# The last cross attention of a decoder: where the causal mask is added to the scores

## The reference

```
q = (queries @ Wq + bq).reshape(B, L, H, dk)      # queries: layernorm(x), 16 x 112 x 256; H = 16, dk = 16
k = (keys @ Wk + bk).reshape(B, S, H, dk)         # keys, values: the context
v = (values @ Wv + bv).reshape(B, S, H, dk)
scores = jnp.einsum('blhd,bshd->bhls', q, k)
causal = jnp.triu(jnp.ones((L, S), dtype=bool), k=1)
scores = jnp.where(causal[None, None], -jnp.inf, scores)
attn = jax.nn.softmax(scores / sqrt(dk), axis=-1)
out = jnp.einsum('bhls,bshd->blhd', attn, v).reshape(B, L, H * dk) @ Wo + bo
```

## Time and profile before

| | us |
|---|---|
| median of three runs | 1831.58 |
| profiled execution | 1840.86 |
| its span | 1839.1 |
| TensorE busy in the span | 1663.2 (90%) |
| VectorE busy | 925.9 (50%) |
| ScalarE busy | 870.3 (47%) |
| GpSimd busy | 336.3 (18%) |

### The profile page before, as it was taken

The page is one execution under the profiler, slowest core; times in us unless marked ns, Lnnn a source line. Parts: engine busy times, 40 slices in busy tenths (PEclk is TensorE's granted clock), DMA queues, the critical chain, the costliest instruction groups (busy, mean ns, idle before and its releaser), DMA issues. The chain is left out here.

```text
span 1839.1 us, 32803 instructions
## 1 busy us (share of the span) xinstructions
PE 1663.2 (90%) x12682; PEld 1091.1 (59%) x12682; DVE 925.9 (50%) x1898; ACT 870.3 (47%) x1780; POOL 336.3 (18%) x304
## 2 busy tenths in 40 slices
PE   7999999799889999989899999999797988699965
PEld 3455555555456656656565899998354666466632
DVE  5566666321656665656433211211464766377747
ACT  5243434333555565665431122222265878256655
POOL 0012112121100000000008400001702544101112
PEclk9999999899999999999979999999897999799978
DMA  7000000100200000000025599996378331000001
GB/s 246 1 1 1 1 1 1 48 5 1 80 18 18 10 18 18 10 18 2 2 65 203 181 330 328 323 330 206 113 181 203 89 83 42 21 12 12 2 1 41
DMA packets 147914, 150.03 MB, mean 82 GB/s; under 512 B 69760, under 2 KB 134976, under 8 KB 147760
## 3 DMA queue, kind: packets, MB, share of 16 engines
q1 hardware_dynamic: 144688, 140.59, 25.0%
q0 software_dynamic: 3072, 7.34, 1.3%
HBM read 120.39 MB, written 27.53 MB: 80 GB/s over the span
## 5 line engine op out<-in xcount | busy, mean ns | idle before, releaser
L906 DVE CUSTOM_DVE_ANT_0 x_probs<-psum,masked 112x439 f32<-112x439 f32 x256 | 142.1, 612 | 71.5 <-PE psum L748 70.7
L759 PE MATMUL psum<-ident,x_probs 112*125 112x112 f32 (+1 forms) x1024 | 142.6, 278 | 28.4 <-DVE x_turned L913 24.6
L759 PEld LDWEIGHTS psum<-ident,x_probs 112*125 112x125 f32 (+1 forms) x1024 | 117.2, 169 | 85.7 <-issue 40.2
L846 ACT ACTIVATE x_probs<-x_probs,x_negmax 112x439 f32<-112x439 f32 x256 | 155.1, 658 | 8.2 <-DVE x_negmax L906 8.2
L2302 DVE TENSOR_TENSOR masked<-masked 128x512 f32<-128x512 f32 x70 | 49.9, 712 | 200.9 <-ACT masked L2204 200.9
L2145 PEld LDWEIGHTS psum<-mix_xb,mix_up 128*128 128x128 f32 x1120 | 130.6, 192 | 2.1 <-issue 0.4
L2145 PE MATMUL psum<-mix_xb,mix_up 128*128 128x128 f32 x1120 | 130.7, 275 | 0.0
L852 ACT COPY x_turned<-psum 125x448 f32<-125x448 f32 x128 | 67.8, 530 | 129.9 <-PE psum L759 128.9
L2155 PE MATMUL psum<-mix_down,masked 128*128 128x256 f32 x560 | 127.0, 380 | 0.1
L1389 PE MATMUL psum<-fold_full,hT 128*112 128x512 f32 x256 | 113.8, 597 | 1.3 <-DVE fold_part L1697 1.3
L2155 PEld LDWEIGHTS psum<-mix_down,masked 128*128 128x128 f32 x560 | 103.5, 190 | 13.4 <-DVE masked L2302 0.4
(11 more groups left out here) (320 smaller groups left out, 3278.7 us busy)
## 6 DMA issues: line engine op xcount, KB each, us to landing
mix_up<-in_moe_up SPq DMA_DIRECT2D x35, 1024.0 KB
mix_down<-in_moe_down SPq DMA_DIRECT2D x35, 1024.0 KB
offset_rows<-join_rows SPq DMA_DIRECT2D x16, 784.0 KB, 5.9
hrow<-offset_rows SPq DMA_DIRECT2D x16, 784.0 KB, 5.3
x_ctx<-in_ctxT SPq DMA_DIRECT2D x16, 375.0 KB, 3.1
slots_x<-masked SPq DMA_DIRECT2D x1, 4480.0 KB, 21.4
mix_rows<-slots_x SPq DMA_DIRECT2D x35, 128.0 KB, 3.0
slots_y<-mix_result SPq DMA_DIRECT2D x35, 128.0 KB, 3.3
```

The lines of the kernel that those rows point to most:

```text
L759: mm = nc.tensor.transpose(psum[0:CHUNK_ROWS[c], 4 + i % 2, k * T:(k + 1) * T], probs[:, n % 2, slot_of_head(HG * g + k), c * CHUNK:c * CH ...
L846: nc.scalar.activation(probs[:, n % 2, slot], probs[:, n % 2, slot], ACT.Exp, bias=negmax[:, n % 2, slot:slot + 1], scale=-1.0).then_inc(e ...
L906: nc.vector.tensor_tensor_reduce(probs[:, n % 2, slot], psum[0:T, slot % 4, 0:KEYS], masked[0:T, n * KEYS:(n + 1) * KEYS], -1.0, -3.0 * NE ...
```

## The change

VectorE now adds the mask, and TensorE no longer does in this stage. In each block of four heads, VectorE runs one `tensor_tensor_reduce` per head in the place of the one maximum per block. It reads the 112 columns of the head's scores from PSUM, adds the mask, multiplies by -1 and writes the result, the negated masked score, to `probs` in SBUF; with the same instruction it finds the minimum over the columns, which is the negated maximum, and a second small instruction writes it to `rowmax`. (With the factor -1 and the starting value 3e30 for the minimum this is the form that the memory attention has already, in `mask_and_largest`, L902, with 439 columns.) `shift` then takes the negated scores from SBUF instead of the scores from PSUM, and ScalarE's exponent has a scale of -1.

On TensorE the mask products are gone from this stage; the first attention keeps them. The score products are the first into their banks (start=True). Since VectorE's first instruction has the scores out of PSUM, the banks are free after `maxed` instead of `shifted`. The new instruction writes `probs`, so it waits for the turns of batch n-2, as `shift` does.

```diff
-        banks_free = factored if offset else shifted
+        banks_free = factored if offset else maxed if causal else shifted
...
-                    if not offset:
+                    if future:
                         nc.tensor.matmul(psum[0:T, r, 0:G], identb[0:T, 0:T], maskb[:], start=True, stop=False, skip_group_check=True)
...
-                        mm = nc.tensor.matmul(psum[0:T, r, k * T:(k + 1) * T], q, kT[rows, g % 2, m, t:t + T], start=offset, stop=True, skip_group_check=not offset)
+                        mm = nc.tensor.matmul(psum[0:T, r, k * T:(k + 1) * T], q, kT[rows, g % 2, m, t:t + T], start=not future, stop=True, skip_group_check=future)
...
-                nc.scalar.activation(x, x, ACT.Exp).then_inc(exped.sem, 1)
+                nc.scalar.activation(x, x, ACT.Exp, scale=-1.0 if causal else 1.0).then_inc(exped.sem, 1)
...
+                elif causal:
+                    dve.wait_ge(*scored.after(At(n), r))
+                    dve.wait_ge(*tile_turned.after(At(n - 2), NG - 1))
+                    for k in range(HG):
+                        found = nc.vector.tensor_tensor_reduce(x[:, k], src[:, k], maskb[:, 0:T], -1.0, -3.0 * NEG, ALU.add, ALU.min, mx[:, k:k + 1])
+                    found.then_inc(maxed.sem, 1)
                 else:
                     dve.wait_ge(*scored.after(At(n), r))
                     nc.vector.tensor_reduce(mx, src, X, ALU.max).then_inc(maxed.sem, 1)
...
-                nc.vector.tensor_tensor(x, src, mx.unsqueeze(2).broadcast_to([T, NG, T]), ALU.subtract).then_inc(shifted.sem, 1)
+                nc.vector.tensor_tensor(x, x if causal else src, mx.unsqueeze(2).broadcast_to([T, NG, T]), ALU.subtract).then_inc(shifted.sem, 1)
```

## The result

The kernel before took 1834.51 us (median of 20 runs), the changed one 1841.7 (20 runs): ratio 1.0042 [1.0027, 1.0056], about 7.7 us slower. That is inside the 0.5% that I called no change, but the interval excludes both no change at all and the small gain that I forecast (1829.5). The time lies in the range of 1822 to 1842, but by luck: the upper end was set for a case, 263 ns per small instruction, that isn't what happened.

The account below looks back on a forecast made before the run. TensorE was taken to set the stage's pace, with VectorE close behind; mask products saved, less VectorE's longer chain (+1.0 us per batch), summed over the batches to -2.2 us, from 1831.6 to 1829.4 (predicted 1829.5), range 1822 to 1842.

Parts of the forecast that it names:

- a case, 263 ns per small instruction: VectorE's small instructions with one fixed part each for instruction and read: +9 us, 1840.7; under a rival of chance 0.18.
- The rival I gave most weight: VectorE's accumulator reads at 112 columns are not hidden: 263 ns gives +9 us, 354 gives +24; chance 0.18.
- the step between the small instructions: VectorE's 112-column mask-and-maximum instructions, with their reads, come 0.197 us apart.
- the chain: VectorE's work per batch, first maximum to next work: four blocks and the shuffle, 6.31 us instead of 5.31.
- The mask's time: TensorE gets back 0.85 us per batch from the removed mask products, at most 13.6 us over 16 batches.
- The walk's three hand-overs: Logarithm, third copy and third mix wait for VectorE's shuffle; output for centring (batches 7, 11, 15); next scores for last block.
- the walk: Batch-by-batch reckoning of the stage: TensorE's mask saving against VectorE's delays, summing to -2.2 us.
- The centring's wait ahead of the output: In batches 7, 11 and 15 TensorE's output waits for VectorE's centring: +0.1 us each, +1.0 in 15.
- new waits for the last maximum: TensorE's next scores wait for VectorE's last maximum, starting 6.88 us after the last ones at the earliest.
- it stays at 0.54: VectorE's subtraction, now reading SBUF instead of PSUM, was taken to keep its 0.54 us.
- One or two of these, +3 to +7: TensorE's clock drops to 1.2 GHz around batches 7, 11, 12, 14: +3 to +7 us; part of the within-0.5% chance, 0.76.
- a step of 0.247: VectorE's small instructions 0.247 us apart instead of 0.197: the walk comes out at +5.5 us.

Follow-up runs that it names:

- e4: Changed kernel with the 64 mask products kept on TensorE beside VectorE's mask; 1.0079 against the kernel before, stage 176.19 us.
- h2: Changed kernel with GpSimd's multiplication cut to 8 columns and useless TensorE products in batches 1 and 2; 1.0009 against the kernel before, stage 160.86 us.
- e2: Changed kernel with GpSimd's multiplication by the inverse denominators cut from 448 columns to 8; 1.0018 against the kernel before, stage 163.45 us.
- e1: Changed kernel with the masked scores written back to PSUM and subtracted from there; 1.006 against the kernel before, stage 168.48 us.
- g1: Changed kernel with only the row maxima put in spare PSUM columns, masked scores in SBUF; 1.0055 against the kernel before, stage 168.27 us.
- g3: Changed kernel with useless TensorE products in pauses at batches 1, 2 and 9; 1.0018 against the kernel before, stage 165.74 us.
- e3: Kernel before without the 64 mask products and without any mask; 0.9972 against the kernel before, stage 155.64 us.
- g2: Changed kernel with row maxima in PSUM and the denominators' shuffle ahead of block 0; 1.0024 against the kernel before, stage 166.17 us.
- h1: Changed kernel with shuffle first, last two subtractions after their maxima, GpSimd's multiplication held back in some batches, useless products before batch 1; 0.9961 against before, stage 154.22 us.
- g4: Changed kernel with row maxima in PSUM, shuffle ahead of block 0, and eight useless products ahead of batch 1's scores; 1.002 against before, stage 165.35 us.
- e6: Kernel before with the shuffle of the denominators moved ahead of block 0 on VectorE; 0.9967 against the kernel before, stage 154.89 us.
- f1: Changed kernel with the shuffle of the denominators moved ahead of block 0 on VectorE; 1.0003 against the kernel before, stage 165.42 us.

## Why the prediction was wrong

**Right.** The rival I gave most weight, that the second instruction of each head counts in full, is false: the step between the small instructions is 0.195 (forecast 0.197), the block 1.43 (1.44), the chain 6.40 (6.31) with one subtraction of 0.73 in it. The mask's time was right (0.85 forecast; 0.7 to 0.8 in e4, 0.87 ahead of batch 0). The walk's three hand-overs hold: where the two causes below are away (h2), the batches without a meeting are within 0.2 us of the walk except 13, which is 0.5 shorter because its output no longer waits for the multiplication that the edit cuts. The centring's wait ahead of the output, new waits for the last maximum, and VectorE's higher busy time are there.

**The step that failed:** "The subtraction now reads SBUF instead of PSUM; with two inputs it has no row at another rate here, so it stays at 0.54." Rate was the wrong question. At 0.54 alone, it takes 1.34 when it comes while GpSimd works on SBUF, because both its operands are there now. It costs 4.3 us (e2, less what its edit brings by itself), and some 1.6 more where the partner is the sum of squares (batches 6, 10 and 14 over the walk in e2 and h2), through three of the walk's hand-overs: later banks (12 and 14: 7.74 for 6.88), later queries (5), and the third copy in 9. And the trace of before had rows that show it. By line, VectorE's normalisation step with two SBUF operands and GpSimd's addition of the bias:

```profile
L285 DVE TENSOR_TENSOR hT<-hT,sq x24: 1081/1092/1981, 222.2 to 1775.3; 128x896 f32<-128x896 f32 x24
```

```profile
L1849 POOL TENSOR_TENSOR second_result<-second_result,weights x32: 1127/1448/1472, 1406.1 to 1558.8; 112x448 f32<-112x448 f32 x32
```

VectorE's step reaches 1981 at a median of 1092, GpSimd's addition has 1127 at the least and 1448 at the median, and neither reads PSUM. Their places in the trace fit: the step of 1981 starts 0.10 us after a GpSimd multiplication of 1.14, and the 18 additions of 1445 ns or more all start 0.16 us after a VectorE addition with two SBUF operands, while none of the other 14 (at most 1147 ns) does. I read means and steps of VectorE, never the spread, and looked for no row of GpSimd at all. That 14 multiplications stood beside the chain before too and lengthened no subtraction is explained by its PSUM operand: the same is shown by e1 and g1.

The Trainium skill ("SBUF — State Buffer", "SBUF: two separate sides") has the rule: VectorE and GpSimd share a pair of ports that is "an exclusive lock, not a bandwidth split", and a VectorE instruction with two SBUF inputs and a GpSimd one that reads SBUF block each other for the whole instruction, whichever starts first. The trace agrees: GpSimd's instruction runs from 1677.63 to 1678.77, the subtraction is recorded from 1677.82, and the work behind it starts at 1679.17, within 0.15 us of 1678.77 + 0.54; and where GpSimd comes second it is the one that takes longer (its sum of squares in batches 6, 10 and 14 takes 1.51 instead of 1.14).

**The clock.** The second failed step: this was a rival ("One or two of these, +3 to +7") that I left out of the sum, and it came true: 3.4 us in batches 1 and 2 (g3), 1.5 at the end (an output of 4.76 for 3.29). I placed it at 7, 11, 12 and 14; it came in 1, 2, 9 and 15. The longest waits of TensorE there are 2.0 (ahead of batch 1's scores), 1.5, 1.8 and 3.3 us, where before they were 0.8, 0.6, 0.6 and 1.65. e3 shows that it needs nothing of VectorE's new work, nor a meeting. The length of one wait alone doesn't decide: the scores of batches 13 and 15 wait 1.7 and keep the clock, those of batch 15 in g2 wait 2.4 and keep it, and in e3 it falls behind a wait of 1.3 (batches 2 and 9).

**The sum of the miss.** Of the 11.6 us, 4.3 are the meetings with the multiplication, 3.4 the clock in batches 1 and 2, 1.6 the meetings with the sum of squares and 1.5 the slow output of batch 15. The first two are what an edit took away; the last two are read off against the walk. The 0.8 left are spread over batches that are each within 0.25 us.

**Slips in the working.** 8.47 + 3.15 is 11.62, not 11.64. By +7 us per +0.05 us a step of 0.247 comes out at +4.8, not +5.5 (and the forecast's "0.247 ns" are us). Neither moves the forecast.

**Open.** What decides whether a pause costs the clock stays open: eight products ahead of batch 1's scores kept it at 1.00 in g3, h1 and h2 and not in g4. Whether batch 15's output could run at the full clock wasn't tried. Each kernel has one profiled execution, so whether the clock falls at the same places in its other executions isn't shown; but batch 1 is at 1.00 in the kernel before and in e6, and below it in all ten other kernels that have no filling.

## What to carry to other kernels

Moving an operand from PSUM to SBUF is not free where GpSimd works beside it: look up every GpSimd instruction of the stage on the timeline, and in the rows by line look at the maximum beside the median, since a group with two clusters can tell of two engines that hold each other up. Work that is removed from TensorE in a stage with pauses is worth what the next chain leaves (here 8.1 of 13.6 us outside three batches), and the pauses that remain can cost its clock (here 4.0 of the 8.1 back); so first look for the hand-over that ends the pauses. Here moving one shuffle ahead of a block (e6) gave nearly all that the whole rebuilt change (h1) did.

## What the runs showed of the hardware

- An instruction with two SBUF inputs on VectorE (448 columns, 0.62) takes 1.42 to 1.60 when it begins within 0.2 us of the start of GpSimd's multiplication of 1.14, less when it begins later (f1: 1.31 at 0.3 us, 0.93 at 0.7); with one operand in PSUM it takes 0.62 to 0.63 in all 64 cases of e1 and of g1, 17 and 16 of which begin beside a GpSimd instruction. A GpSimd instruction of 1.14 that comes second takes 1.51.
- The accumulating instruction on 112 columns comes every 0.195 us with its read, SBUF as target; with the result (e1) or only the maximum (g1) in PSUM every 0.23, and the read takes 140 ns instead of 83.
- TensorE's clock fell to 1.2 GHz in batches in which it had waited 1.3 to 3.3 us at one place, though not behind all such waits (2.4 in g2). Eight products of the mask without use (1.67 us) ahead of batch 1's scores made that batch 1.9 us shorter (g3).
